# DLRM tower on one core: gates on the gathers, one ScalarE copy moved, fewer waits on TensorE, another orientation of the last layer

## What is computed

```python
e = jnp.stack([tbl_0[ids[:, 0]], ..., tbl_26[ids[:, 26]]], axis=1)      # 512 x 27 x 128
interactions = jnp.einsum('bnd,bmd->bnm', e, e)
i, j = jnp.triu_indices(27, k=1)
z = interactions[:, i, j]                                               # 512 x 351
h = jnp.concatenate([z, dense_ctx], axis=1)                             # 512 x 367
h = jnp.maximum(h @ W_top1 + b_top1, 0.0)                               # 512 x 512
h = jnp.maximum(h @ W_top2 + b_top2, 0.0)                               # 512 x 256
y = h @ W_top3                                                          # 512 x 1
```

## Time and profile before

| | |
|---|---|
| median of 3 runs | 110.33 us |
| the profiled execution | 109.96 us |
| its span, first to last instruction | 107.8 us |
| granted clock of TensorE | 1.00 throughout |
| PE, DVE, ACT, POOL busy | 92%, 68%, 65%, 61% of the span |
| chain that ended last | PE 43%, DVE 37%, issue 9%, DMA 8% |
| 61 gathers on POOL | 63.6 us busy, 1.04 us in the mean |

### The profile page before, as it was taken

How to read it: one execution, slowest core, us unless ns; L and a number is a source line. 1 busy time by engine, 2 the same in 40 slices (tenths; PEclk the granted TensorE clock), 3 DMA queues, 4 the chain that set the end, 5 groups by cost and what they waited for, 6 DMA issues and landing times.

```text
span 107.8 us, 2420 instructions
## 1 busy us (share of the span) xinstructions
PE 99.6 (92%) x993; PEld 84.2 (78%) x993; DVE 73.8 (68%) x68; ACT 70.4 (65%) x100; POOL 65.9 (61%) x71
## 2 busy tenths in 40 slices
PE   4995999999999799999999879999999999997992
PEld 4993887777767687876778679999998897996790
DVE  3299999999999999999999943035245405622131
ACT  5039999999999999999999956144404241421021
POOL 3177788777787777787777787777777720005000
PEclk9999999999999999999999999999999999999999
DMA  1899688888869694869526412679653443034100
GB/s 42 192 365 340 167 301 292 207 257 300 223 250 250 193 305 135 239 207 222 177 49 204 185 49 55 213 131 253 222 93 78 150 128 53 9 132 81 24 0 1
DMA packets 13031, 18.26 MB, mean 169 GB/s; under 512 B 7601, under 2 KB 8446, under 8 KB 13020
## 3 DMA queue, kind: packets, MB, share of 16 engines
q1 hardware_dynamic: 9552, 12.90, 39.8%
q0 software_dynamic: 2016, 4.06, 13.8%
q10 hardware_dynamic: 1452, 1.14, 3.5%
HBM read 16.32 MB, written 1.77 MB: 168 GB/s over the span
## 4 chain that ended last, share of the span: by engine, by line
PE 43%; DVE 37%; issue 9%; DMA 8%; ACT 1%; SPq 0%; ACTq 0%; DVEq 0%
DVE hot L474 25%; PE psG L359 13%; DVE parts L479 10%; PE psG L340 8%; PE psG L386 5%; PE psH L402 5%; PE psT L318 4%; DMA pick_ids<-in_picked_ids 4%; PE psH L340 3%; PE psH L371 3%; DMA pair_grams<-gram 3%; DMA zT<-pair_grams 2%; PE psH L417 1%; DVE hot L460 1%; DVE hot L463 1%
## 5 line engine op out<-in xcount | busy, mean ns | idle before, releaser
L301 POOL DMA_INDIRECT rows<-in_tbl,ids_sb x61 | 63.6, 1042 | 21.7 <-issue 18.3
L340 PE MATMUL psG<-hot,parts 128*128 128x512 f32 x196 | 49.5, 401 | 2.4 <-ACT hot L564 1.2
L340 PEld LDWEIGHTS psG<-hot,parts 128*128 128x128 f32 x196 | 35.2, 188 | 13.5 <-DVE hot L474 4.8
L474 DVE TENSOR_TENSOR hot<-pick_ids,psH 128x1536 fp32r<-128x1536 int32 (+2 forms) x23 | 41.5, 1843 | 0.0
L560 ACT ACTIVATE hot<-pick_ids,row_no 128x512 fp32r<-128x512 int32 (+1 forms) x30 | 19.4, 710 | 0.0
L479 DVE TENSOR_TENSOR parts<-table,parts 128x1024 fp32r<-128x1024 f32 (+1 forms) x12 | 16.2, 1349 | 0.0
L564 ACT ACTIVATE hot<-hot 128x1024 fp32r<-128x1024 f32 (+2 forms) x12 | 15.0, 1247 | 0.4
L359 PEld LDWEIGHTS psG<-ET 128*54 128x54 f32 x512 | 13.3, 130 | 2.3 <-issue 1.6
L359 PE MATMUL psG<-ET 128*54 128x54 f32 x512 | 13.9, 213 | 1.3 <-issue 1.2
L487 DVE COPY gram<-psG 128x432 f32<-128x432 f32 x8 | 7.3, 911 | 10.8 <-PE psG L359 10.8
L571 ACT COPY gram<-psG 128x432 f32<-128x432 f32 x8 | 7.3, 914 | 11.2 <-PE psG L359 10.5
(11 more groups left out here) (31 smaller groups left out, 49.7 us busy)
## 6 DMA issues: line engine op xcount, KB each, us to landing
table<-in_tbl SPq DMA_DIRECT2D x6, 640.0 KB, 4.8
table<-in_tbl SPq DMA_DIRECT2D x6, 512.0 KB, 5.5
pick_ids<-in_picked_ids SPq DMA_DIRECT2D x11, 256.0 KB, 4.0
rows<-in_tbl,ids_sb POOLq DMA_INDIRECT x61, 3.8
pair_grams<-gram SPq DMA_DIRECT2D x4, 216.0 KB, 2.3
pair_grams<-gram ACTq DMA_DIRECT2D x4, 216.0 KB, 3.0
w_sb<-in_w SPq DMA_DIRECT2D x1, 768.0 KB, 4.4
w_sb<-in_w SPq DMA_DIRECT2D x1, 512.0 KB, 4.3
```

The costliest lines, as they stand in the source:

```text
L301: pool.indirect_dma_start(out=rows[:, n % RING, x, :], out_offset=None, in_=gathered_tables[f], in_offset=bass.IndirectOffsetOnAxis(ap=ids ...
L340: last = pe.matmul(picked_psum(k), parts[:, k % 2, x, c, :], hot[:, k % 2, c, looked_up(k)], start=x == 0 and c == 0, stop=x == 1 and c == ...
L474: dve.tensor_tensor(hot[:, k % 2, first:end, looked_up(k)], pick_ids[:, k % TABLES, looked_up(k)].unsqueeze(1).to_broadcast(shape), number ...
```

## The change

1. POOL waits for TensorE before 20 of the gathers: before gathers 7, 9, 12, 15, 18, 21, 25, 29, 33, 37, 41 and 48 until 1, 2, ... 12 picks are done; before 44, 45, 50, 51, 57 and 59 until units 0 to 5 are done; before 54 until layer 1 of tile 0 is done, before 56 until layer 2 of tile 0 is.
2. For pick 11 alone, ACT's second step on the last one-hot blocks stands behind the copy of pick 10.
3. TensorE waits once where a semaphore's value was waited for again and again: three waits fewer per block group in a pick's high half, none in the second output half of layer 2.
4. Layer 3 of tiles 0 to 2 has the samples (`h2`) stationary and the single column `w3` moving; the result is a column of 128, copied to `y_cols`. These 384 results go out in a DMA of their own, once tile 2 is done; the last tile's 128 follow alone at the end.

```diff
+    BEHIND_PICKS = [7, 9, 12, 15, 18, 21, 25, 29, 33, 37, 41, 48]
+    BEHIND_UNITS = [44, 45, 50, 51, 57, 59]
+    BEHIND_LAYERS = [54, 56]
...
-            return psH[0:1, 0 if t == T - 1 else 1, 3, :]
+            return psH[0:1, 0, 3, :] if t == T - 1 else psH[:, 1, 3, 0:1]
...
+            sp.wait_ge(y_ready, T - 1)
+            sp.dma_start(out[0:B - P, :].rearrange("(t p) o -> p (t o)", p=P), y_cols[:, :], allow_slow_non_contiguous=True).then_inc(out_done, 16)
             sp.wait_ge(y_ready, T)
-            sp.dma_start(out.rearrange("b o -> o b"), y_sb[:, :]).then_inc(out_done, 16)
-            sp.wait_ge(out_done, 16)
+            sp.dma_start(out[B - P:B, :].rearrange("p o -> o p"), y_sb).then_inc(out_done, 16)
+            sp.wait_ge(out_done, 32)
...
                 for x, f in enumerate(quad(t, q)):
+                    if number in BEHIND_PICKS:
+                        pool.wait_ge(picked, BEHIND_PICKS.index(number) + 1)
+                    if number in BEHIND_UNITS:
+                        pool.wait_ge(multiplied[H - 1], 2 * (BEHIND_UNITS.index(number) + 1))
+                    if number == BEHIND_LAYERS[0]:
+                        pool.wait_ge(l1_done, N1)
+                    if number == BEHIND_LAYERS[1]:
+                        pool.wait_ge(l2_done, N2)
...
                         if x == 0:
-                            own = CH[k] - BY_ACT[k]
-                            if c < own:
-                                pe.wait_ge(hot_ready, 2 * k + (1 if c < HOT_SPLIT else 2))
-                            else:
+                            if c in (0, HOT_SPLIT):
+                                pe.wait_ge(hot_ready, 2 * k + (1 if c == 0 else 2))
+                            elif c == CH[k] - BY_ACT[k]:
                                 pe.wait_ge(last_hot_ready, k + 1)
...
-                    pe.wait_ge(h1_dve if k < 2 else h1_act, 2 * t + 1 + k % 2)
+                    if n == 0:
+                        pe.wait_ge(h1_dve if k < 2 else h1_act, 2 * t + 1 + k % 2)
...
-                    last = pe.matmul(y_psum(t), w3_sb[:, k:k + 1], h2[:, k, :], start=k == 0, stop=k == N2 - 1)
+                    if t < T - 1:
+                        last = pe.matmul(y_psum(t), h2[:, k, :], w3_sb[:, k:k + 1], start=k == 0, stop=k == N2 - 1)
+                    else:
+                        last = pe.matmul(y_psum(t), w3_sb[:, k:k + 1], h2[:, k, :], start=k == 0, stop=k == N2 - 1)
...
             for x in range(FP - 1):
                 split_high(x + 1)
                 make_last_hot(x + 1)
+                if x + 1 < FP - 1:
+                    finish_last_hot(x + 1)
                 pick_copy(x)
+                if x + 1 == FP - 1:
+                    finish_last_hot(x + 1)
```

More of the change, by code:

```diff
@@ L109, in dlrm_tower @@
         h2 = sb("h2", [P, N2, P])
-        y_sb = table[0:1, 0, 0:B // D, :].rearrange("o a d -> o (a d)")
+        y_sb = table[0:1, 0, 0, 0:P]
+        y_cols = sb("y_cols", [P, T - 1])
         psT = pb("psT", [P, 2, 4, P])
@@ L295, in _ @@
             pool.wait_ge(ids_in, 16)
+            number = 0
             for n in range(T * NQ):
@@ L304, in _ @@
                     ).then_inc(gathered[t][q], 16)
+                    number += 1
             wait_written(pool, T - 1)
@@ L506, in take_y @@
                 dve.wait_ge(l3_done, t + 1)
-                dve.tensor_copy(y_sb[:, P * t:P * (t + 1)], y_psum(t)).then_inc(y_ready, 1)
+                dve.tensor_copy(y_sb if t == T - 1 else y_cols[:, t:t + 1], y_psum(t)).then_inc(y_ready, 1)
             dve.memset(psG[:, :, 1, :], 0.0).then_inc(banks_zero, 1)
@@ L557, in make_last_hot, with finish_last_hot @@
                 act.wait_ge(pick_ids_in[k], 16)
-                chunks = range(CH[k] - BY_ACT[k], CH[k])
-                for c in chunks:
+                for c in range(CH[k] - BY_ACT[k], CH[k]):
                     act.activation(hot[:, k % 2, c, looked_up(k)], pick_ids[:, k % TABLES, looked_up(k)], ACT.Abs, bias=row_number(k, c),
                                    scale=-1.0).then_inc(distance_ready, 1)
+            def finish_last_hot(k):
                 act.wait_ge(distance_ready, sum(BY_ACT[:k + 1]))
-                last = hot[:, k % 2, chunks[0]:CH[k], looked_up(k)]
+                last = hot[:, k % 2, CH[k] - BY_ACT[k]:CH[k], looked_up(k)]
                 act.activation(last, last, ACT.Relu, bias=1.0, scale=-1.0).then_inc(last_hot_ready, 1)
@@ L598, in _ @@
             make_last_hot(0)
+            finish_last_hot(0)
             for x in range(FP - 1):
```

## The result

The changed kernel takes 111.77 us (median of 4 runs, 110.83 to 112.38); the kernel before, timed beside it, 110.28 (4 runs, 109.29 to 110.46). The ratio is 1.0164, interval 1.0111 to 1.0217: slower by 1.1% to 2.2%, where 0.68 us less was forecast. Timed again in another set of runs, it is 1.0059 (1.0022 to 1.0096). Its profiled execution took 110.83 us with a span of 109.0; that of before 109.96 and 107.8.

A forecast was written before the change was run, and what follows sets the result against it. DVE bounds the kernel up to 56 us, PE is the path from 61. Terms −1.00 − 0.03 + 0.35 = −0.68 us, so the median goes from 110.33 to 109.65; own range 109.4 to 109.95, 8 in 10 within 109.2 to 110.25.

The forecast's parts named there:

- ScalarE's copy ahead: Ahead of the first unit: ACT copies pick 10 once it is done, the moved `Relu` stays hidden; gain 1.00 us.
- Fewer waits: TensorE in pick 10: seven waits at 0.004 us saved, gain 0.03 us, bounds 0 and 0.05; layer 2, 0.
- Layer 3 turned round: Layer 3 of tiles 0 to 2: saving on moving columns is paid in stationary ones; 0 at the end.
- The gates: POOL's gathers: awaited steps are already done, so gates hold nothing; 0, bounds 0 and 0.05 us each, 1.0 by gather 60.
- What is late next: Quad 15, before unit 6: PE, 1.03 us earlier, waits for gather 60; 0.35 us given back, 0.68 gain left.
- Output: Early DMA of 384 results: hidden under 5.8 us of cover, landing in 1.9 to 2.6; 0, bounds −0.1 and +0.1.
- The 384 short writes are slow: Rival at the output: the writes take over 5.8 us, each us beyond counts in full; 111 or more; 4 in 100.
- a final wait for the first output DMA: Sign at the kernel's end: a last wait for the early output DMA would make the prediction wrong; no size given.

The follow-up runs named there:

- gates_alone: The kernel before with part 1 only, the 20 gates: 109.25 us, ratio 0.9983 (0.9941 to 1.0025).
- output_alone: The kernel before with part 4 only, layer 3 turned round and the early output DMA: 111.36 us, ratio 1.0131.
- tile_2_only: The changed kernel with only tile 2's 128 results in the early DMA, side by side; tiles 0 and 1 not written: 110.2 us, ratio 1.0015.
- spread: The changed kernel with its 384 early results sent 512 bytes apart to a scratch tensor: 123.24 us (kernel before 150.06); again, 109.09 us, ratio 0.9964.
- near_inside: The changed kernel with its 384 early results written 4 bytes apart into its own tensor, not the output: 124.97 us, ratio 0.8331 (kernel before 149.75).
- output_by_tile_2: The changed kernel with tiles 0 and 1 (256 results) sent early after tile 1, tile 2's 128 by themselves; second timing: 116.17 us, ratio 1.0533.
- old_output: The changed kernel with part 4 undone: 123.40 us, ratio 0.8225 (kernel before 150.06); again, 109.39 us, ratio 0.9985.
- no_gates: The changed kernel without gates and part 4, leaving parts 2 and 3: 108.99 us, ratio 0.9956; again, 109.03 us, ratio 0.9934.

## Why the prediction was wrong

- **ScalarE's copy ahead** held: 60.91 forecast for the copy, 60.87 measured; the unit at 61.57, measured 61.59. The `Relu` was hidden: ACT's first unit copy started at 63.55 (63.53). (The forecast's 63.46 for the end of the quad copies leaves out that each begins some 0.1 us ahead of the end of the one before; as a plain sum it is 63.55, past the 63.53, and measured it is 63.45.) The slices show DVE full to the 23rd, not the 22nd; nothing hangs on it.
- **Fewer waits** can't be told from the start of pick 10: it ran 56.07 to 60.86 in the chain before and 56.02 to 60.84 after, 4.79 and 4.82 us. 0.03 us less was forecast, and nothing of that size can be tested here.
- **Layer 3 turned round** held: 0.54 against 0.53 us, by the load of 128 columns at 190 ns. By "TensorE: Matmul & The Clock Gate" of the Trainium skill, section "LDWEIGHTS (loading the stationary operand)", a load costs its columns, and the trace agrees in kind: one of 128 columns takes 190 ns, one of one column 80, and the four follow each other at 0.11 us.
- **The gates** held where the kernel before takes 110 us: POOL's gaps stayed 0.30 us (0.31 in a few), gather 60 was issued at 86.00, and gates_alone measured 0.9983. Of the 1.0 us that I kept as a bound nothing came that can be told.
- **What is late next** held in kind: quad 15's loads at 88.58 against 88.67, unit 6 at 89.72 against 89.83. Its sizes did not: PE was 0.92 earlier at quad 14 and not 1.03, 0.18 and not 0.35 was given back at quad 15, unit 6 was 0.79 earlier, and 0.11 more went on the way to the last copy, at the last `zT`. That these come to −0.68 again is luck. Over many executions the step is softer than one sum makes it: gather 60 landed in 2.5 to 4.3 us in the profiles here, and the kernels with the copy moved and a quick output gained 0.15% to 0.66% (0.2 to 0.7 us) in six timings, in two of which the interval reaches past 1.
- **Output** failed. The step said that the 384 results are hidden, 5.8 us of cover over a DMA of 1.9 to 2.6 us, "I take 0, bounds −0.1 and +0.1". Measured: last confirmed 9.2 us after the issue, and +1.9 us in SyncE's last wait (+0.9 to +1.4 in the repeats, the changed kernel's and output_alone). It is the rival "The 384 short writes are slow", which had 4 in 100 and the right threshold; its 111 fits 111.77, and a final wait for the first output DMA was named as a sign of being wrong. My error was the row: 416 short pieces of L193 are **reads** of memory into the chip, of 128 bytes each, and I let them stand for **writes** of 4 bytes to memory that lie side by side. The bounds should have gone up to several us, since no row of the kernel before shows such a write. The rule that I quoted against the edit, one descriptor per element, was right (400 packets more in the queue: 384 and 16 confirmations), and I set it aside with that row. The number of packets is not what costs, though, as tile_2_only and spread show.

What the runs show of the cause: 4-byte writes that lie 4 bytes apart are confirmed late, the last 8.1 to 9.2 us after the issue, 128 of them nearly as late as 384, and in the output or in a tensor of the kernel's own alike (near_inside); at 64 bytes apart all 384 are confirmed in 1.7 us. So neither count nor destination decides, but how close the pieces lie. The length of the stretch that matters is not shown: between 4 and 64 bytes no spacing was tried. In 64 bytes lie 16 pieces of the changed kernel and five of the 12-byte form, which is in time and still shows 3.8 us in one run. "DMA: Bandwidth & Descriptors" of the Trainium skill, section "Specifications", says that below 512 bytes the engines read, modify and write. The runs agree only in part: 4 bytes at 64 apart are below it as well, and quick. Writes that must take turns at one place would explain both, but that was argued and not shown.

Adding up: −0.68 + 1.9 = +1.2 in the profiled spans. The medians stand 1.5 apart: the spans of the changed kernel's four executions are 109.0 to 109.7, and in three of them 2.5 to 2.75 us lie outside the span, where it is 1.8 in the profiled one; what that is stays open. In the repeat, with a wait of 1.8, the medians are 0.74 apart.

Open: why close writes are confirmed late; why engines stand still in output_by_tile_2; and why parts 1 to 3 give 18% where the kernel before takes 150 us (17% on the second such chip, with other early outputs). There TensorE has pauses in its units and the gates do hold POOL back, but the kernel before has no trace there, and gates, copy and waits weren't tried one by one. I can't say which it was.

The version to keep is old_output, parts 1 to 3 with the output as a row in one DMA at the end: it is 18% quicker where the kernel before takes 150 us, and at 110 us it costs nothing that can be told (109.39 against 109.70). no_gates has lower medians at 110 us (108.99 and 109.03, against 109.39 in another set), but it was never run at 150 us, and the gates alone showed no loss.

## What to carry to other kernels

A DMA's landing is judged only by rows of the same direction and the same piece: a read of 128-byte pieces says nothing of a write of 4-byte ones. Results that stand as a column across partitions are best sent as a row (last wait 0.9 us here), or at least 64 bytes apart. Pieces of 12 bytes side by side were in time too, with 6 us of cover and a last confirmation at 2.2 and 3.8 us. In single words side by side they are sent at once, and the last is confirmed 8 to 9 us after the issue. Where a step has no row of its kind, the bounds must be wide enough for its threshold, here 5.8 us, to lie inside.

## What the runs showed of the hardware

- Packets sent and DMA confirmed are two things: the early DMA's packets were gone 1.2 us after the issue, its last confirmation came at 9.2 us.
- While such writes are pending, an instruction packet of 16 KB takes 2.7 to 4.0 us instead of 0.9 to 1.4. Issued in the middle of the work (output_by_tile_2), they go with a stop of ACT and DVE for some 6 us, and of PE behind them for 3.6 to 3.8. TensorE's granted clock then falls, by the page's slices of 2.9 us:

```profile
PEclk9999999999999999999999999999999999855599
```

  0.5 of full speed is the lower of its two levels (1.2 GHz), from about 99.5 to 108.5 us, after an idle PE from 95.9 to 99.5 us.
- The same program, the kernel before, takes 110 us on some chips (sets two to four) and 150 on others (the first and the last set), where TensorE's mean granted clock is 0.85 to 0.89 and not 1.00.
